# Splitting the attention output and the expert rows on GpSimd, and turning the output by DMA

## The reference

```python
# attention, 16 heads of 16
attn = softmax(q @ k.T / sqrt(16))
coh = sigmoid(tanh(concat(x, cs) @ Wc1.T + bc1) @ Wc2.T + bc2)    # per query and head
mod = attn * coh[..., None]
mod = mod / (mod.sum(-1) + 1e-8)
fa = softmax(fp @ pe.T)                                           # one row per sequence
out = ((1 - 0.21) * mod + 0.21 * fa) @ v
x = x + out @ Wout.T + bout
# experts: 8 of them, the best two for each row
gate = softmax(rms(x) @ wg_W + wg_b + genre @ gg_W + gg_b)
cw = the two largest of gate, 0 elsewhere
h1 = relu(x @ W1 + b1); h2 = relu(h1 @ W2 + b2)                   # 256 -> 512 -> 512
x = x + sum over experts of cw * (h2 @ W3 + b3)                   # 512 -> 256
```

## Time and profile before

| | before |
|---|---|
| median of three runs | 969.85 us |
| the profiled execution: its span, all of its time | 969.8 us |
| PE busy | 886.2 us, 91% |
| DVE / POOL / ACT busy | 726.9 / 595.2 / 530.2 us |
| mean granted TensorE clock | 0.964 of full |
| batches 1 to 6 start at | 106.3, 163.6, 222.4, 279.7, 337.3, 394.6 us |
| batch 7, and the first expert tile | 452.4, 525.5 us |

### The profile page before, as it was taken

One profiled execution on the slowest core, in us unless ns is written; L12 is line 12 of the kernel. 1 busy time (PEld: TensorE's weight loads), 2 busy tenths in 40 slices (PEclk: granted clock), 3 DMA queues, 4 the chain that ended last, 5 costly groups with the idle time before them and its releaser, 6 DMA issues. The chain is left out here.

```text
span 969.8 us, 23388 instructions
## 1 busy us (share of the span) xinstructions
PE 886.2 (91%) x6806; PEld 511.9 (53%) x6807; DVE 726.9 (75%) x1530; ACT 530.2 (55%) x1100; POOL 595.2 (61%) x750
## 2 busy tenths in 40 slices
PE   5799999999999999998979889989899999999883
PEld 2233333333333333332324777868778888888662
DVE  7878888898988999899895876848765665665531
ACT  3268787778878787885687545323233333323220
POOL 4413345646556555542443699877998878877653
PEclk9999999999999999998787998989999999999998
DMA  6562353526326152530344785853343334334321
GB/s 212 116 97 69 63 97 78 87 86 113 111 62 145 60 103 69 99 85 14 124 146 153 254 241 137 217 125 58 64 73 53 50 45 59 52 45 60 50 42 18
DMA packets 109547, 92.87 MB, mean 96 GB/s; under 512 B 63816, under 2 KB 102088, under 8 KB 107152
## 3 DMA queue, kind: packets, MB, share of 16 engines
q1 hardware_dynamic: 95776, 72.51, 31.6%
q0 software_dynamic: 13296, 18.23, 11.4%
q10 hardware_dynamic: 384, 0.97, 0.3%
HBM read 49.46 MB, written 37.77 MB: 90 GB/s over the span
## 5 line engine op out<-in xcount | busy, mean ns | idle before, releaser
L1258 DVE TENSOR_REDUCE mx<-bank 128x1 f32<-128x512 f32 x512 | 324.4, 683 | 39.7 <-PE bank L834 33.8
L1146 ACT ACTIVATE arena<-bank 128x512 f32<-128x512 f32 x512 | 277.3, 596 | 65.6 <-PE bank L845 63.1
L1180 ACT ACTIVATE hf<-bank,small 128x256 f32<-128x256 f32 (+1 forms) x312 | 126.7, 452 | 267.0 <-PE bank L1013 214.7
L708 POOL TENSOR_TENSOR hl<-hf,hh 128x256 f16<-128x256 f32 (+1 forms) x312 | 220.2, 1009 | 74.1 <-DVE y_dest L1536 44.6
L1518 DVE CAST hh<-hf 128x256 f16<-128x256 f32 (+1 forms) x312 | 152.9, 522 | 114.8 <-ACT hf L1180 108.5
L1013 PE MATMUL bank<-hh,arena 128*128 128x256 f16 (+1 forms) x1248 | 204.6, 267 | 11.9 <-POOL hl L708 6.4
L834 PE MATMUL bank<-arena 48*128 48x512 f16 x512 | 170.1, 393 | 14.3 <-DVE mx L1258 12.3
L845 PE MATMUL bank<-arena 49*128 49x512 f16 x512 | 166.1, 396 | 15.0 <-ACT arena L1146 6.9
L1013 PE MATMUL bank<-hl,arena 128*128 128x256 f16 (+1 forms) x624 | 165.4, 265 | 0.0
L1013 PEld LDWEIGHTS bank<-hh,arena 128*128 x1248 | 122.1, 98 | 42.5 <-issue 22.4
L858 PE MATMUL bank<-arena 128*17 128x512 f32 x1024 | 142.3, 629 | 0.9 <-ACT arena L1146 0.9
(11 more groups left out here) (228 smaller groups left out, 957.4 us busy)
## 6 DMA issues: line engine op xcount, KB each, us to landing
raw<-in_we SPq DMA_DIRECT2D x16, 1024.0 KB
arena<-parts_dram SPq DMA_DIRECT2D x84, 128.0 KB
parts_dram<-arena SPq DMA_DIRECT2D x64, 128.0 KB, 3.7
xs<-in_pads SPq DMA_DIRECT2D x8, 816.0 KB, 7.0
arena<-in_xT SPq DMA_DIRECT2D x8, 512.0 KB, 4.5
arena<-in_x SPq DMA_DIRECT2D x8, 512.0 KB, 6.2
out<-rows SPq DMA_DIRECT2D x8, 512.0 KB, 5.3
arena<-parts_dram SPq DMA_DIRECT2D x24, 64.0 KB, 2.8
```

The lines of the kernel that those rows point to most:

```text
L708: nc.gpsimd.tensor_tensor(hl[which][:, par, m, 0:n], hf[which][:, m, 0:n], hh[which][:, par, m, 0:n], ALU.subtract).then_inc(lo[which], 1)
L1146: nc.scalar.activation(pr[:, s % TT, n, :], b_bank[no % B_RING][:, :], ACT.Exp, scale=SCALE).then_inc(b_read, 1)
L1180: nc.scalar.activation(hf[which][:, m, 0:n], layer[which][m // 2][:, m % 2 * TS:m % 2 * TS + n], ACT.Relu, bias=bias[which][:, bass.ds(e, ...
L1258: V.tensor_reduce(mx[:, g % 2, c, s % TT:s % TT + 1], a_bank[no % A_RING][:, :], X, ALU.max).then_inc(a_read, 1)
```

## The change

- Tasks `at` 0 and 1 go. GpSimd splits each half of `att` into `att_parts` after its `fade` (`split_output`, a cast and a subtraction on [128, 512]): half 0 in slot 12, half 1 in slot 2 of the next batch, right behind `fade`. SyncE turns the parts with one transposing DMA of 256 KB for each half (`turn_output`): half 0 at slot 13, half 1 at slot 4 behind the reads of the stacks. `op` waits for both DMAs. A half's parts are written again only after the DMA of the batch before has landed.
- `op` 0 to 3 move from slots 3, 4, 5, 6 to 4, 5, 6, 7; `c1` 0 from slot 7 to 11; squares, logits, routing, the scatters and some additions move by up to a slot or two.
- `vs` is copied by ACT, not DVE. The splitting of rows (`send_rows`, two halves in slots 7 and 11) goes from ACT and DVE to GpSimd, but for the last batch.
- The scaling of the maxima (L1264) becomes an operation on two tensors in SBUF: `mx` times a constant times a tensor of ones.
- Routing: in step 1 the first expert is found by `logit < 0` on the lowered logits, with no maximum of `gate`, so six steps become five; what is added to the key is `numbers()` as eighths (a tensor of its own).
- For the last batch half 1 is split by ACT and DVE in expert tile 1 and turned by SyncE behind one weight load.

The diff, cut to its core ("..." where lines are left out; renamed semaphores and their declarations are among these):

```diff
@@ -148,30 +148,30 @@
...
-    2: [("at", 1, -1), ("coh", 2, 0)],
-    3: [("coh", 3, 0), ("op", 0, -1)],
-    4: [("op", 1, -1)],
-    5: [("ot", 0, 0), ("op", 2, -1)],
-    6: [("op", 3, -1)],
-    7: [("vs", 0, 0), ("c1", 0, 1)],
+    2: [("coh", 2, 0)],
+    3: [("coh", 3, 0)],
+    4: [("op", 0, -1)],
+    5: [("ot", 0, 0), ("op", 1, -1)],
+    6: [("op", 2, -1)],
+    7: [("op", 3, -1), ("vs", 0, 0)],
...
-    11: [("at", 0, 0), ("v", 1, 1)],
+    11: [("c1", 0, 1), ("v", 1, 1)],
...
-ROUTE_AT = {(9, 0): 0, (10, 1): 1, (11, 0): 2, (11, 1): 3, (12, 0): 4, (13, 1): 5}
+ROUTE_AT = {(9, 1): 0, (11, 0): 1, (11, 1): 2, (12, 0): 3, (13, 1): 4}
...
-BIAS_AT = {14: 14, 15: 15, 0: 16, 2: 18}
-
-SENT_AT = {8: 0, 10: 1}
-
-SCATTER_AT = {15: (31, 0, 1), 0: (32, 1, 2), 3: (35, 2, 4), 4: (36, 4, 6), 6: (38, 6, 8)}
+BIAS_AT = {14: 14, 15: 15, 0: 16, 1: 17}
+
+SENT_AT = {7: 0, 11: 1}
+
+SCATTER_AT = {15: (31, 0, 1), 0: (32, 1, 2), 1: (33, 2, 3), 3: (35, 3, 5), 4: (36, 5, 7), 5: (37, 7, 8)}
...
@@ -179,7 +179,7 @@
...
-TAIL = {0: [("ot", 3)], 1: [("at", 1)], 2: [("op", 0), ("op", 1)], 3: [("op", 2), ("op", 3)], 8: [("count", 0)]}
+TAIL = {0: [("ot", 3)], 2: [("op", 0), ("op", 1)], 3: [("op", 2), ("op", 3)], 8: [("count", 0)]}
...
@@ -287,7 +287,9 @@
...
-    fv, attT = carve(seventh, 0, [P, TT, E]), carve(seventh.bitcast(F16), 2 * TT * E, [P, 2, ET, S])
+    fv, attT = carve(seventh, 0, [P, TT, E]), carve(seventh.bitcast(F16), 2 * TT * E, [P, ET, TT, 2, P])
+    after_v, after_xr = 2 * TT * (H + 1) * (SUM + 1) + TT * E, TT * E + ET * S + TT * (E + NX)
+    att_parts = [carve(r.bitcast(F16), 2 * at_, [P, TT, 2, P]) for r, at_ in ((sixth, after_v), (seventh, after_xr))]
...
@@ -491,6 +495,13 @@
...
+        def turn_output(i, b):
+            sp.wait_ge(att_low[i], b + 1)
+            if b > 0:
+                evicted(sp, ("op", 3, b - 1))
+            sp.dma_start(attT[:, i, :, :, :].rearrange("p t c n -> p (t c) n"),
+                         att_parts[i][:, :, :, :].rearrange("p t c e -> p (t c e)"), transpose=True).then_inc(att_turned[i], 16)
+
...
@@ -527,6 +538,10 @@
...
+            if at == 13 and 0 <= b < B:
+                turn_output(0, b)
+            if at == 4 and 0 <= b - 1 < B:
+                turn_output(1, b - 1)
...
@@ -535,6 +550,7 @@
...
+            if at == 8:
...
@@ -578,6 +594,8 @@
...
+            if now == 1:
+                turn_output(1, B - 1)
...
@@ -618,6 +636,24 @@
...
+
+        def split_output(i, b):
+            c = slice(i * P, (i + 1) * P)
+            pool.wait_ge(faded, 2 * b + i + 1)
+            after(pool, att_turned[i], 16 * b)
+            nc.gpsimd.tensor_copy(att_parts[i][:, :, 0, :], att[:, :, c]).then_inc(att_high[i], 1)
+            pool.wait_ge(att_high[i], b + 1)
+            nc.gpsimd.tensor_tensor(att_parts[i][:, :, 1, :], att[:, :, c], att_parts[i][:, :, 0, :], ALU.subtract)\
+                .then_inc(att_low[i], 1)
+
+        def send_rows(half, b):
+            r = slice(half * TT // 2, (half + 1) * TT // 2)
+            evicted(pool, ("op", r.stop - 1, b))
+            after(pool, scattered, 16 * 2 * TT * b)
+            nc.gpsimd.tensor_copy(sent_parts[:, r, 0, :], rows[:, r, 0:E]).then_inc(sent_high, 1)
+            pool.wait_ge(sent_high, 2 * b + half + 1)
+            nc.gpsimd.tensor_tensor(sent_parts[:, r, 1, :], rows[:, r, 0:E], sent_parts[:, r, 0, :], ALU.subtract)\
+                .then_inc(sent_low, 1)
...
@@ -733,6 +769,7 @@
...
+                split_output(1, b - 1)
...
@@ -748,17 +785,19 @@
...
+                if 0 <= b < B:
+                    field_values(b)
...
-                if 0 <= b < B:
-                    field_values(b)
...
-            if at == 9 and 0 <= b - 1 < B:
+            if at == 10 and 0 <= b - 1 < B:
...
+            if at in SENT_AT and 0 <= b - 1 < B:
+                send_rows(SENT_AT[at], b - 1)
...
@@ -766,6 +805,8 @@
...
+            if at == 12 and 0 <= b < B:
+                split_output(0, b)
...
@@ -893,11 +940,9 @@
...
-            elif what == "at":
-                pe.wait_ge(faded, 2 * b + i + 1)
...
-                evicted(pe, ("at", 0, b))
-                evicted(pe, ("at", 1, b))
+                for e in range(ET):
+                    pe.wait_ge(att_turned[e], 16 * (b + 1))
...
@@ -971,12 +1016,9 @@
...
-            elif what == "at":
-                last = turned(m, lambda t2: att[:, t2, i * P:(i + 1) * P])
...
-                r = slice(i * P, (i + 1) * P)
...
-                    last = thirds(m[:, 0:E + NX], wox_high[:, e, :], wox_low[:, e, :], attT[:, 0, e, r], attT[:, 1, e, r],
+                    last = thirds(m[:, 0:E + NX], wox_high[:, e, :], wox_low[:, e, :], attT[:, e, i, 0, :], attT[:, e, i, 1, :],
...
@@ -1113,9 +1155,10 @@
...
-            elif what == "at":
+            elif what == "vs":
...
-                nc.scalar.activation(attT[:, 0, i, :], m[:, :], ACT.Copy).then_inc(att_high, 1)
+                after(act, fv_set, b)
+                nc.scalar.activation(vsum[:, :], m[:, 0:E], ACT.Copy).then_inc(done, 1)
...
@@ -1164,11 +1207,16 @@
...
-        def send_high(half, b):
+        def send_last_high(half):
...
-            evicted(act, ("op", r.stop - 1, b))
-            after(act, scattered, 16 * 2 * TT * b)
+            evicted(act, ("op", r.stop - 1, B - 1))
+            act.wait_ge(scattered, 16 * 2 * TT * (B - 1))
...
+
+        def split_last_high():
+            act.wait_ge(faded, 2 * B)
+            act.wait_ge(att_turned[1], 16 * (B - 1))
+            nc.scalar.activation(att_parts[1][:, :, 0, :], att[:, :, P:E], ACT.Copy).then_inc(att_high[1], 1)
...
@@ -1201,14 +1249,12 @@
...
-            if 4 <= at < 8 and 0 <= b - 1 < B:
-                square_rows(at - 4, b - 1)
-            if at in (8, 9) and 0 <= b - 1 < B:
-                send_high(at - 8, b - 1)
-            elif at == 10 and 0 <= b - 1 < B:
-                weigh(b - 1)
+            if 5 <= at < 9 and 0 <= b - 1 < B:
+                square_rows(at - 5, b - 1)
...
+            if at == 10 and 0 <= b - 1 < B:
+                weigh(b - 1)
...
@@ -1226,14 +1272,14 @@
...
-            if now == 2:
-                take(("at", 1, B - 1))
+            if now == 1:
+                split_last_high()
...
-                send_high(0, B - 1)
-                send_high(1, B - 1)
+                send_last_high(0)
+                send_last_high(1)
...
@@ -1261,8 +1307,10 @@
...
-            V.tensor_scalar(mxp[:, g % 2, 0:G * TT], mx[:, g % 2, :, :].rearrange("p h t -> p (h t)"), -1.0 / SHIFT_UNIT, None, ALU.mult)\
-                .then_inc(mx_split, 1)
+            if g == 0:
+                dve.wait_ge(cleared, 1)
+            V.scalar_tensor_tensor(mxp[:, g % 2, 0:G * TT], mx[:, g % 2, :, :].rearrange("p h t -> p (h t)"),
+                                   -1.0 / SHIFT_UNIT, ones[:, 0:G * TT], ALU.mult, ALU.mult).then_inc(mx_split, 1)
...
@@ -1324,16 +1372,12 @@
...
-            elif what == "vs":
-                after(dve, fv_set, b)
-                V.tensor_copy(vsum[:, :], m[:, 0:E]).then_inc(done, 1)
-            elif what == "at":
-                dve.wait_ge(att_high, ET * b + i + 1)
-                V.tensor_tensor(attT[:, 1, i, :], m[:, :], attT[:, 0, i, :], ALU.subtract).then_inc(done, 1)
...
+                after(dve, sent_low, 2 * b)
+                after(dve, logits_set, 2 * b)
...
@@ -1345,6 +1389,7 @@
...
+                after(dve, att_low[i // 2], b)
...
@@ -1356,7 +1401,7 @@
...
-            return w["count"][:, None, 0:NX].to_broadcast([P, TT, NX])
+            return eighths[:, None, :].to_broadcast([P, TT, NX])
...
@@ -1366,23 +1411,20 @@
...
+                V.scalar_tensor_tensor(key[:, :, :], logit[:, :, :], 0.0, numbers(), ALU.is_lt, ALU.add)
...
-                chain(V.tensor_reduce(top[:, 0, :], gate[:, :, :], X, ALU.max))
+                chain(V.tensor_reduce(first_key[:, :], key[:, :, :], X, ALU.min))
...
-                chain(V.tensor_tensor(key[:, :, :], gate[:, :, :], over_experts(top[:, 0, :]), ALU.is_lt))
-                chain(V.scalar_tensor_tensor(key[:, :, :], key[:, :, :], float(NX), numbers(), ALU.mult, ALU.add))
-                chain(V.tensor_reduce(first_key[:, :], key[:, :, :], X, ALU.min))
-            elif step == 3:
...
-                chain(V.tensor_reduce(top[:, 1, :], left[:, :, :], X, ALU.max))
-            elif step == 4:
-                chain(V.tensor_tensor(key[:, :, :], left[:, :, :], over_experts(top[:, 1, :]), ALU.is_lt))
-                chain(V.scalar_tensor_tensor(key[:, :, :], key[:, :, :], float(NX), numbers(), ALU.mult, ALU.add))
+                chain(V.tensor_reduce(top[:, :], left[:, :, :], X, ALU.max))
+            elif step == 3:
+                chain(V.tensor_tensor(key[:, :, :], left[:, :, :], over_experts(top), ALU.is_lt))
+                chain(V.tensor_tensor(key[:, :, :], key[:, :, :], numbers(), ALU.add))
...
-            elif step == 5:
+            elif step == 4:
...
@@ -1504,9 +1546,13 @@
...
-        def send_low(half, b):
```

(34 more changed lines are left out.)

16 lines of the change are left out of this document (8 added, 8 removed).

## The result

The changed kernel took 999.92 us (median of four runs, 997.60 to 1001.25) against 971.55 for the one before in the same comparison: 1.0302 of it, 95% interval 1.0271 to 1.0334. One of the four runs of the kernel before took 3524.18 us and stays out of the ratio. The change makes the kernel 3% slower; I had forecast 982 and no change that can be measured, with 996 as the upper end. The profiled execution has a span of 998.1 us, 28.3 more than before.

A forecast was written before the change was run, and what follows sets the result against it. Attention was taken as bound by PE, with DVE close behind. From 969.8 us: six batches at 0.0, first batch -1.0, last +0.5, clock falls +12.5, giving 981.8, so 982 us; range 959 to 996.

The forecast's parts named there:

- the landing: End of half 1's turning DMA, which `op` 0 awaits: 10.9 us after slot 2, between 9.9 and 11.6.
- the bound of 11.6: Latest landing after slot 2: four stack reads ahead done at 9.6, then 256 KB more in 1.9 us.
- the lower bound: Landing at 9.9 us after slot 2: DMA issued at 6.8 on an empty queue, 3.1 us with the semaphore.
- The stalls given back: PE's waits from slot 5 to the next slot 2, shortened by 1.3 us for DVE and GpSimd, 0.6 for ACT.
- The clock's price: Granted clock falls to 0.50 around slot 4's waits: 2.5 us lost each, in 5 of 7 batches, +12.5 us.
- The rival of the port: DVE operations on two SBUF tensors blocked by GpSimd up to 0.5 us each, 1.3 us a batch lost: 990 us; chance 0.06.
- First and last batch: First batch waits for no DMA, -1.0 us; last has its DMA behind two weight loads, +0.5 us (0 to +4).
- The slow rival: Lower clock lasts 13.7 us a fall, costing 5.3 us, not 2.5: 990 us with three, 1006 with seven; chance 0.14.

## Why the prediction was wrong, point by point

**The mechanism was right.** Every place was named: the DMA issued 6.8 us after slot 2 (6.9 in batches 2 to 4; in batches 1, 5 and 6 the small DMA of the maxima ahead of it took 2.7 to 4.1 us instead of 2.3, and it was 8.6, 7.9 and 7.4), the parts ready at 4.3 (4.4), PE standing still ahead of `op` 0, the clock falling in that wait, DVE near 48 (49) and POOL near 40 (40.1) us a batch.

**The step that failed is the landing.** I put it at 10.9, with 11.6 as its upper end; it was 13.5 to 13.9 in batches 2 to 6 and 14.5 in batch 1. The upper end was built from "the four that lie ahead ... are done at 9.6 or so" and "256 KB more take 1.9 us", as if a DMA ended when its share of the bytes had passed. The bytes came out nearly as forecast: the sum has them through 4.8 us after the issue, and the last packet ended after 4.8 to 5.3 in batches 1 to 6. What the bound of 11.6 left at nothing is the time from the last packet to the last semaphore update. It is 0.5 us when the DMA is alone, and was inside the 3.1 of the lower bound; here it was 0.6 to 1.8. And I took 10.9, below a bound that had no term for it. With reads ahead and behind, 7.0 us went from issue to the last update in batch 4; with nothing but the two stores ahead of it, 3.6. The 256 KB, the reads and GpSimd's scatters share the engines, and PE waits for the last of the updates: in batch 4 the first came 5.6 us after issue and the last 7.0. But the spread is not the delay: in batch 5 the 16 updates came at 5.4 to 5.6, and the first of them was 5.4 us or more behind the issue in all six batches, against 3.0 alone. The reads ahead are shown to be the cause of most of it by moving them; the reads behind cost 0.4, and what the scatters cost was not separated. The Trainium skill's page DMA: Bandwidth & Descriptors, section Queues, rings and completion order, has a rule that fits: a DMA is spread over up to 16 rings, and each ring's semaphore increment lands only after every earlier write of that DMA engine. The trace agrees so far that the last update came 0.6 to 1.8 us after the last packet among this traffic and 0.5 after it alone; it does not tell which writes an update waited for.

**The same step was missing for the other DMAs of the queue.** I priced the stack reads for one reader and took the small DMAs of the maxima as fixed. Moving the reads showed that it is one queue with three readers in slots 2 to 8, each of whom pays for what was issued shortly before it.

**The stalls given back were more than I took**: slot 5 to the next slot 2 takes 44.8 us at the full clock where my sum was 45.6 and before had 47.25. With 3.0 us from the landing, -0.8 from here and 2.5 for a fall of the clock, a batch forecast at 57.3 comes to 62.0, which is what was measured.

**The clock's price was right, 2.5 us, its count was not.** I expected falls in 5 of the 7 batches that wait, since I had the idle time cut in two. In batches 2 to 4 slot 4 did not wait for the stores, and `op` 0 waited 5.5 to 5.8 us in one piece; in batches 1, 5 and 6 the idle time was in two pieces, 1.6 to 2.3 us for the stores and 3.0 to 4.2 for the DMA. The clock was low in or next to the wait for the DMA in all seven batches.

**GpSimd, the port, the maxima.** GpSimd at 40 of 62 us was no bound. The rival of the port had the right behaviour and the wrong price. DVE operations do stop for GpSimd, and how long depends on where they fall: the comparison with `eighths` in step 1 has a median of 1.09 us and a shortest of 0.18, and the comparison that it stands for had a median of 0.52 before. Its row, and its place in batch 4 beside the GpSimd subtraction that it waits for:

```profile
L1414 DVE SCALAR_TENSOR_TENSOR key<-logit,eighths x8: 176/1085/1087, 152.7 to 650.9; 128x32 f32<-128x32 f32 x8
```

```profile
338.84 1.09 DVE L1414 SCALAR_TENSOR_TENSOR key<-logit,eighths 128x32 f32<-128x32 f32 x1
338.72 1.16 POOL L631 TENSOR_TENSOR arena<-arena 128x512 f16<-128x512 f32 x1
```

It ends at 339.93, 0.05 us after the subtraction, and does so in each of batches 1 to 5. But the loss that the rival put on it, the 1.3 us of stalls a batch not given back, is not there: more was given back than I took (above). The maxima edit does nothing, as costed, because the old form stops for GpSimd as well.

**First and last batch.** Batch 0 gained 1.7 (I said 1.0). Its start at 51.0 and not 48.3 I had not looked at; but in kernels with the same code up to there it lay between 48.3 and 53.8, with the clock low for 7 to 20 us of that time, so this is no effect of the change that I can name. In the last batch PE waited 8.6 us for the DMA, where I had 3.0; the DMA landed 9.2 us after its issue, where the forecast has 7.3. The whole stretch, with the first expert tile, lost 4.2, just above the 0 to 4 that I gave the batch. The tail gave 2.8 back, which I did not predict.

**The slow rival** had the right direction and not the cause: its falls of the clock last 13.7 us, and here they lasted 10.2 at most. The kernel is slower by a later landing, which I had ruled out with a bound. A range that reached to 996 was 4 us short because the bound of an unmeasured wait came from bytes over rate alone.

## What to carry to other kernels

Here the readers of one DMA queue waited for whatever was issued shortly before their own DMA. So before a new DMA that an engine waits for goes into it, list what is issued ahead of it, and put everything that is needed late behind it and behind the next small DMA as well. Here four reads cost 33 us when they went from slot 3 to slot 1, and four others gave 12 us (16 by the ratios) when they went from slot 4 to slot 6. Count the end of a DMA from its last semaphore update, not from its last byte. When work is taken off several engines, undo each part in the final kernel as well as adding each alone: here neither relief showed by itself.

## What was not expected of the hardware

- A transposing DMA of the maxima (2.3 us alone) took 6.95 us until the stores behind it were issued, with eight reads of 128 KB issued before it, the last of them 2.7 us before.
- The time of a 256 KB transposing DMA from SBUF to SBUF was 3.1 us from issue to the last update alone, what I had taken from the one out of DRAM, and 5.6 to 7.0 behind four reads. Of the 7.0 in batch 4, 1.8 passed after the last packet had ended.
- A DVE operation on 128x16 values, 0.17 us alone, took 0.75 us beside a GpSimd addition that ran meanwhile and ended 0.04 us after it, with one tensor in SBUF as its input as well as with two.
- Kernels with equal code up to there start attention at 48.3 to 53.8 us, which is more than most parts of this change are worth. The four latest (52.5 to 53.8) have the clock low for 20.5 us before it, the others for 6.8 to 10.2.
